# An expert-choice search without work between its steps, one pass of places, and shared experts beside the scatter

## The chip, the cores and the metric

The kernel runs on one NeuronCore of one Trainium2 chip. The metric is the device time of one execution in microseconds (us), lower is better; the time before is the median of three runs. Engines: PE is TensorE, DVE is VectorE, ACT is ScalarE, POOL is GpSimd, SP is the engine that issues most of the DMAs. TensorE runs at one of two levels, 1.2 or 2.4 GHz; the trace gives the granted clock of a stretch as a share of full speed, so that 0.50 is 1.2 GHz and 1.00 is 2.4 GHz.

## The reference

A two-layer decoder on x of shape (4, 512, 128), float32. Each layer is x + attention(norm x), x + cross-attention(norm x), x + feed-forward(norm x). The change touches only the feed-forward of layer 0, a mixture of 16 routed experts and 2 shared ones over 2048 tokens:

```python
logits = flat @ gate_w                                   # (2048, 16)
scores = jax.nn.softmax(logits.astype(jnp.float32), -1) + gate_b
_, topi = jax.lax.top_k(scores, K)                       # K = 2
weights = jnp.take_along_axis(logits, topi, axis=-1) * ROUTE_SCALE
capacity = math.ceil(N * K / n_experts * 1.25)           # 320

def per_expert(gid, w1, w3, w2):
    match = topi == gid
    assigned = match.any(-1)
    w_tok = jnp.sum(jnp.where(match, weights, 0.0), -1)
    wm = jnp.where(assigned, w_tok, -jnp.inf)
    vals, idx = jax.lax.top_k(wm, capacity)
    valid = assigned[idx]
    xs = flat[idx]
    y = _swiglu(xs, w1, w3, w2) * jnp.where(valid, vals, 0.0)[:, None]
    return (idx, y)
out = jnp.zeros_like(flat).at[idxs.reshape(-1)].add(ys.reshape(-1, Dx))
shared = jax.vmap(lambda w1, w3, w2: _swiglu(flat, w1, w3, w2))(sw1, sw3, sw2)
out = out + shared.mean(0)
```

Each expert takes, of the tokens that chose it, the 320 with the largest logit; between equal logits the earlier token wins.

## The kernel before, in words

Each engine has a program of its own, written by hand in the order in which it runs; semaphores (`wait_ge`, `then_inc`) tie the programs together. On DVE the helper `link` makes every instruction of a chain wait for the one before it; `blink` does the same inside the search loop. The stages of layer 0 follow one another: attention, cross-attention, then the feed-forward, and after it layer 1. X (128 partitions x 16 tiles x 128) is the residual, hT the normalised input with tokens along the columns. A token tile is 128 tokens, a batch is four tiles.

The feed-forward of layer 0 goes like this:

- **Norm and router.** DVE normalises 16 tiles (L1545). PE transposes them (L975), four to a bank of PSUM, ACT copies each bank to hT (L712). Then PE makes the logits, 16 matmuls with the tokens as weights (L1189), each passed twice since the data is float32.
- **Top two.** A DVE chain over 128x256 tiles: softmax, first and second choice, then `g_wm`, the logit where the token chose the expert and -1e30 elsewhere. PE transposes g_wm, so that the 16 experts lie along partitions (`g_wmT`), and POOL takes the maximum over all partitions (L567).
- **The search.** For each expert a threshold is sought between `g_lo` (at least 320 values reach it) and `g_hi` (fewer do). There are 16 steps, as a loop of 4 turns with 4 steps each. One step on DVE: three cuts (`g_try`, L1791), three comparisons of 256 values (L1794), a sum over the three results (`g_ge_cnt`, L1796), then, beside PE's work, three small instructions that lower g_hi (L1777 to L1779, `lower_end`); PE adds the counts of an expert's partitions (L1265, 3 columns); DVE tests them (L1799), counts the full cuts (L1800), raises g_lo (L1801) and divides the width by four (L1802). Behind its own matmul of each step PE runs one "guest": one unit of the shared experts, `shared_up` (L1197, two matmuls of 512 columns), and in half of the steps a half of `shared_down` (L1208, 8 matmuls of 128 columns). ACT takes Silu of one bank (L820) and copies the other (L821), POOL multiplies the two (L577) and adds the results to X (L586, L589).
- **The places.** Both ends go back to token order through PE (L1272). A token at or above g_hi is sure, one between the ends is tied. `places` counts how many came before: PE multiplies the mask by a triangle and by ones (L1281, L1282), DVE adds up the sums of the 16 tiles one after another (L1823, x15), then adds the triangle's result (L1824). It runs once for the tied tokens, to see which of them still fit, and once for those taken, to give them rows. Two casts write the rows (`g_row`, L1843), the second raises g_chain to 200.
- **The scatter.** POOL waits for g_chain 200 and issues 32 indirect DMAs (L596), which write the token rows to `xs_rows` in HBM, expert by expert; SP loads them back (L467), PE transposes them (L1218) and the routed experts run: L1228 up, L1238 down, four experts to a turn.

## Time and profile before

| what | value |
|---|---|
| median of 3 runs | 1634.54 us (1625.73 to 1634.92) |
| the profiled execution | 1623.32 us, its span 1621.5 us |
| granted TensorE clock, mean over the span | 0.903 |
| PE busy | 1384.9 us, 85% |
| DVE busy | 1001.7 us, 62% |
| ACT busy | 733.1 us, 45% |
| POOL busy | 565.8 us, 35% |
| the chain that ended last | PE 77%, DVE 12%, issue 3%, ACT 2%, POOL 2%, DMA 1% |

Busy shares are averages over all stages. Between 669 and 840 us after the span's start, the stretch of this feed-forward up to the first routed matmul, the engines take turns; that stretch is read from the trace row by row. "Idle" in brackets behind a row is the time for which the engine had nothing before it, and what ended it.

### The profile page before, as it was taken

To read this page: it belongs to the slowest core of one execution; us is meant where nothing else is said; L and a number is where in the kernel's file an instruction comes from. 1 tells how busy PE (TensorE), PEld (TensorE's weight loads), DVE (VectorE), ACT (ScalarE), POOL (GpSimd) and SP (SyncE) were. 2 spreads that over 40 slices of the span, in tenths; PEclk is the share of its full clock that TensorE was granted. 3 is DMA by queue.
4 is the path that set the end of the run, shared out by engine and by line. 5 is a ranking of instruction groups with operands and counts; after the bars stand their busy time and mean duration, and the time that the engine had idled before them with its cause. 6 is when DMAs were issued, how large, how long until landed. Compare 5 with 4: busy or idle time off the path is not lost.

```text
span 1621.5 us, 30956 instructions
## 1 busy us (share of the span) xinstructions
PE 1384.9 (85%) x10924; PEld 963.9 (59%) x10924; DVE 1001.7 (62%) x2374; ACT 733.1 (45%) x1487; POOL 565.8 (35%) x568
## 2 busy tenths in 40 slices
PE   4999999999999699557229458989989999949998
PEld 2566666666666466434127336766766776738887
DVE  2576676676666676488303328686786777755554
ACT  2566666666666365212003125554554555523222
POOL 1455555555555000023441236532332334211210
PEclk7899999999999899578659759999998999969999
DMA  3323100100000200000013224211211211000000
GB/s 129 113 82 100 34 26 31 34 23 34 34 23 23 59 2 1 0 1 1 7 38 98 47 48 117 54 47 28 41 48 26 41 47 29 21 1 1 0 0 26
DMA packets 91918, 61.36 MB, mean 38 GB/s; under 512 B 26841, under 2 KB 78890, under 8 KB 91830
## 3 DMA queue, kind: packets, MB, share of 16 engines
q1 hardware_dynamic: 89782, 58.88, 13.1%
q0 software_dynamic: 2048, 1.27, 0.3%
q8 instruction: 59, 0.97, 0.3%
q14 instruction: 29, 0.24, 0.1%
HBM read 21.63 MB, written 10.49 MB: 20 GB/s over the span
## 4 chain that ended last, share of the span: by engine, by line
PE 77%; DVE 12%; issue 3%; ACT 2%; POOL 2%; DMA 1%; SPq 1%; DVEq 0%; POOLq 0%; ACTq 0%
PE psum L1033 8%; PE psum L1378 8%; PE psum L1046 7%; PE psum L1023 7%; PE psum L1369 6%; PE psum L1500 6%; PE psum L1363 4%; PE psum L1390 4%; PE psum L1482 4%; PE psum L1228 2%; PE psum L1000 2%; PE psum L1009 2%; PE psum L1053 2%; PE psum L1004 2%; POOL xs_rows L596 2%
## 5 line engine op out<-in xcount | busy, mean ns | idle before, releaser
L561 POOL TENSOR_TENSOR arena<-arena,rden 128x512 f32<-128x512 f32 x256 | 260.8, 1040 | 253.1 <-DVE rden L1586 253.1
L755 ACT ACTIVATE arena<-psum,negmax 128x512 f32<-128x512 f32 x256 | 173.6, 683 | 136.2 <-DVE negmax L1577 134.9
L1959 DVE TENSOR_REDUCE negmax<-psum 128x1 f32<-128x512 f32 x256 | 165.2, 686 | 88.4 <-PE psum L1369 88.1
L1577 DVE TENSOR_REDUCE negmax<-psum 128x1 f32<-128x512 f32 x256 | 164.3, 684 | 11.2 <-PE psum L1023 7.7
L1033 PE MATMUL psum<-cst,arena 128*128 128x128 f32 x1024 | 143.9, 280 | 1.4 <-DVE arena L1572 0.5
L1033 PEld LDWEIGHTS psum<-cst,arena 128*128 128x128 f32 x1024 | 109.0, 141 | 52.8 <-issue 50.9
L1023 PE MATMUL psum<-a_qk 64*128 64x512 f32 x768 | 124.9, 430 | 0.0
L1369 PE MATMUL psum<-w,wqkv 128*64 128x208 f32 x1024 | 123.8, 365 | 0.0
L637 POOL TENSOR_TENSOR a_qblk<-a_qstack,cst 96x512 fp32r<-96x512 f32 x64 | 68.4, 1069 | 145.4 <-PE psum L1369 136.4
L1363 PE MATMUL psum<-a_kstack,a_qblk 96*128 96x512 f32 x256 | 99.2, 469 | 16.7 <-DMA a_kstack<-a_klo 16.7
L916 ACT ACTIVATE kT<-psum,negmax 128x512 f32<-128x512 f32 x64 | 44.0, 687 | 136.2 <-PE psum L1378 97.3
L1023 PEld LDWEIGHTS psum<-a_qk 64*128 64x128 f32 x768 | 63.0, 187 | 70.7 <-issue 59.9
L1500 PE MATMUL psum<-f_h,f_w 128*128 128x512 f32 x384 | 99.2, 407 | 1.5 <-DVE arena L2048 0.8
L1369 PEld LDWEIGHTS psum<-w,wqkv 128*64 128x64 f32 x1024 | 64.3, 141 | 58.6 <-issue 49.1
L1963 DVE COPY arena<-psum 128x512 f32<-128x512 f32 x128 | 87.2, 682 | 2.1 <-PE psum L1378 2.1
L953 ACT ACTIVATE arena<-psum 128x512 f32<-128x512 f32 x64 | 38.2, 597 | 104.3 <-PE psum L1500 104.3
L916 ACT ACTIVATE hst<-psum,negmax 128x512 f32<-128x512 f32 x64 | 44.0, 687 | 86.7 <-PE psum L1378 52.5
L1500 PEld LDWEIGHTS psum<-f_h,f_w 128*128 128x128 f32 x384 | 70.5, 191 | 18.8 <-DVE arena L2048 3.5
L910 ACT ACTIVATE arena<-psum 128x512 f32<-128x512 f32 x128 | 76.3, 596 | 1.6 <-PE psum L1378 1.6
L2048 DVE TENSOR_TENSOR arena<-psum,arena 128x512 f32<-128x512 f32 x64 | 44.2, 691 | 47.3 <-ACT arena L953 47.2
L1590 DVE SCALAR_TENSOR_TENSOR a_qk<-psum,a_qk 128x512 fp32r<-128x512 f32 x32 | 22.1, 692 | 74.3 <-ACT a_qk L732 74.3
L640 POOL TENSOR_TENSOR wqkv<-big_k,cst 128x512 f32<-128x512 f32 x64 | 67.3, 1052 | 0.0
(306 smaller groups left out, 2828.5 us busy)
## 6 DMA issues: line engine op xcount, KB each, us to landing
hst<-hT SPq DMA_DIRECT2D x32, 256.0 KB, 2.3
a_kstack<-a_khi SPq DMA_DIRECT2D x128, 64.0 KB, 2.0
wst<-wqkv SPq DMA_DIRECT2D x32, 192.0 KB, 2.4
w<-in_ew SPq DMA_DIRECT2D x2, 2048.0 KB, 8.6
a_kstack<-a_klo SPq DMA_DIRECT2D x64, 64.0 KB, 2.0
xs_rows<-f SPq DMA_DIRECT2D x3, 1024.0 KB, 5.6
arena<-xs_rows SPq DMA_DIRECT2D x8, 384.0 KB, 3.5
ys_rows<-wqkv SPq DMA_DIRECT2D x8, 384.0 KB, 2.6
```

Source lines behind the costliest of these rows:

```text
L561: pool.tensor_tensor(a0_p[u % 4], a0_p[u % 4], rden[:, u:u + 1].broadcast_to([P, SEQ]), ALU.mult).then_inc(a0_norm, 1)
L755: act.activation(a0_p[u % 4], bank[u % 4][:, :], ACT.Exp, bias=negmax[:, u:u + 1], accum_out=den[:, u:u + 1]).then_inc(a0_exp, 1)
L916: act.activation(ptile[n % 4], bank[n % 4][:, :], ACT.Exp, bias=negmax[:, n % 8:n % 8 + 1]).then_inc(a1_exp, 1)
L1023: mm = pe.matmul(bank[2 * (p % 2) + h][:, :], a0_qk[par][r:r + DK, q, p * P:(p + 1) * P], a0_qk[par][r:r + DK, k, :], start=(i == 0), stop ...
L1033: mm = pe.transpose(bank[4 + u % 2][:, kt * P:(kt + 1) * P], a0_p[u % 4][:, kt * P:(kt + 1) * P], ident)
L1046: mm = pe.matmul(bank[7][h * DK:(h + 1) * DK, qs], a0_vtok[par][:, kt, h * DK:(h + 1) * DK], a0_pT[par][h][:, kt, qs], start=(kt == 0), st ...
L1363: pe.matmul(bank[n % 4][:, :], qblk[:, hg, j, lg:lg + 2, :, :].rearrange("p g h l -> p (g h l)"), kstack[it % 2][:, n // 4, :], start=True ...
L1369: mm = pe.matmul(bank[n % 4][blk * HQ * LG:(blk + 1) * HQ * LG, first_key:first_key + WIN], rblk[:, hg, j, g, :, :].rearrange("p h l -> p ...
L1378: mm = pe.transpose(bank[4 + n % 2][:, kt * P:(kt + 1) * P], ptile[n % 4][:, kt * P:(kt + 1) * P], ident)
L1500: mm = pe.matmul(bank[2 * (u % 2) + w][:, :], w_parts[:, e, wp, w * FF + hf * P:w * FF + (hf + 1) * P], h_parts[hp][:, c * SEQ:(c + 1) * S ...
L1577: dve.tensor_reduce(negmax[:, u:u + 1], bank[u % 4][:, :], AX.X, ALU.max, negate=True).then_inc(a0_max, 1)
L1959: dve.tensor_reduce(negmax[:, n % 8:n % 8 + 1], bank[n % 4][:, :], AX.X, ALU.max, negate=True).then_inc(a1_max, 1)
```

## The change

Five edits, all in layer 0's feed-forward:

1. **Router by batch.** PE makes the logits of a batch behind the transposes of the next one, rather than all behind all.
2. **Mask.** g_wm is made with two instructions in place of three (a minimum of the logit and +-1e30).
3. **Search.** The guests are gone. Each comparison sums its own result (a second operation and an output for the accumulator), so that L1796 goes; the test of the counts sums too, so that L1800 goes; the width is divided while PE works.
4. **Places.** Sure and tied tokens lie side by side in one tile (`g_kind`, 512 columns), and one pass counts both: ones first, then the triangle. A tied token stands behind all sure ones (`g_back`); its place alone tells whether it fits.
5. **Shared experts.** All 16 units run behind the places' matmuls on PE, Silu on ACT, and the multiply and the add to X on DVE, both straight from PSUM, after g_chain 200. The ACT copies and POOL's multiplies are gone. The product tile now has two buffers (arena 1 and 2). POOL's memsets and its two staging copies stand ahead of its maximum.

```diff
             for i in range(BISECT):
                 pe.wait_ge(b_count, i + 1)
                 pe.matmul(bank[2][:, 0:CUTS], same_expert, g_ge_cnt[:, :], start=True, stop=True).then_inc(b_total, 1)
-                shared_up(i)
-                if i >= 4 and i % 4 in (1, 2):
-                    shared_down(i // 4 - 1, i % 4 == 1)
...
             pe.wait_ge(g_chain, 100)
-            pe.matmul(bank[1][:, 0:E0], ones[:, :], g_cnt[:, :], start=True, stop=True)
...
+            kinds = arena[:, 2, 1, :]
+            pe.matmul(bank[3][:, :], ones[:, :], kinds, start=True, stop=True).then_inc(g_mm, 1)
+            pe.matmul(bank[2][:, :], tri, kinds, start=True, stop=True).then_inc(g_mm, 1)
+
+            for u in range(4 * B):
+                shared_up(u)
+                if u >= 4 and u % 4 in (1, 2):
+                    shared_down(u // 4 - 1, u % 4 == 1)
...
                 for k in range(BSTEPS):
                     par = k % 2
...
                     for c in range(CUTS):
-                        ins = dve.tensor_scalar(g_ge[:, c, :], g_wmT[:, :], g_try[:, par, c:c + 1], None, ALU.is_ge)
-                    blink(ins)
-                    dve.tensor_reduce(g_ge_cnt[:, :], g_ge[:, :, :], AX.X, ALU.add).then_inc(b_count, 1)
+                        ins = dve.tensor_scalar(g_ge[:, c, :], g_wmT[:, :], g_try[:, par, c:c + 1], None, ALU.is_ge, ALU.add, g_ge_cnt[:, c:c + 1])
+                    ins.then_inc(b_count, 1)
+                    blink(dve.tensor_scalar(g_step[:, 1 - par:2 - par], g_step[:, par:par + 1], 1.0 / (CUTS + 1), None, ALU.mult))
                     lower_end(1 - par, blink)
                     dve.wait_ge(b_total, i * BSTEPS + k + 1)
-                    blink(dve.tensor_scalar(g_full[:, par, :], bank[2][:, 0:CUTS], CAP - 0.5, None, ALU.is_ge))
-                    blink(dve.tensor_reduce(g_nfull[:, :], g_full[:, par, :], AX.X, ALU.add))
-                    dve.scalar_tensor_tensor(g_lo[:, :], g_nfull[:, :], g_step[:, 0:1], g_lo[:, :], ALU.mult, ALU.add)
-                    blink(dve.tensor_scalar(g_step[:, :], g_step[:, :], 1.0 / (CUTS + 1), None, ALU.mult))
+                    blink(dve.tensor_scalar(g_full[:, par, :], bank[2][:, 0:CUTS], CAP - 0.5, None, ALU.is_ge, ALU.add, g_nfull[:, :]))
+                    blink(dve.scalar_tensor_tensor(g_lo[:, :], g_nfull[:, :], g_step[:, par:par + 1], g_lo[:, :], ALU.mult, ALU.add))
...
+            link(dve.memset(g_slot[:, 0, :, :], 0.0))
             dve.wait_ge(g_mm, 4)
...
+            tot = bank[3][:, :].rearrange("p (t k e) -> p t k e", k=2, e=E0)
+            for t in range(1, NT):
+                link(dve.tensor_tensor(g_slot[:, t, :, :], g_slot[:, t - 1, :, :], tot[:, t - 1, :, :], ALU.add))
+            link(dve.tensor_tensor(g_back[:, :], g_slot[:, NT - 1, 0, :], tot[:, NT - 1, 0, :], ALU.add))
             dve.wait_ge(g_mm, 5)
...
+            link(dve.tensor_tensor(g_slot[:, :, :, :], g_slot[:, :, :, :], bank[2][:, :].rearrange("p (t k e) -> p t k e", k=2, e=E0), ALU.add))
+            link(dve.tensor_tensor(g_slot[:, :, 1, :], g_slot[:, :, 1, :], bcast(g_back[:, :], 1, NT), ALU.add))
+            link(dve.tensor_tensor(g_slot[:, :, :, :], g_slot[:, :, :, :], g_kind[:, :, :, :], ALU.mult))
+            link(dve.tensor_tensor(g_rt[:, :, :], g_slot[:, :, 0, :], g_slot[:, :, 1, :], ALU.add))
+            link(dve.tensor_scalar(g_sc[:, :, :], g_rt[:, :, :], float(CAP) - 0.5, float(ROWS), ALU.is_ge, ALU.mult))
+            link(dve.tensor_tensor(g_rt[:, :, :], g_rt[:, :, :], g_sc[:, :, :], ALU.add))
+            link(dve.tensor_tensor(g_rt[:, :, :], g_rt[:, :, :], g_wm[:, :, :], ALU.add))
...
+            def shared_hid(u):
+                c = u // 4
+                dve.wait_ge(sh_silu, u + 1)
+                if c >= 2 and u % 4 == 0:
+                    dve.wait_ge(sh_y, c - 1)
+                dve.tensor_tensor(sh_hidden[c % 2][:, u % 4, :], bank[5 + 2 * (u % 2)][:, :], silu[:, u % 2, :], ALU.mult).then_inc(sh_hid, 1)
+
+            def shared_add(c):
+                dve.wait_ge(sh_y, c + 1)
+                xc = X[:, c * QT:(c + 1) * QT, :]
+                dve.scalar_tensor_tensor(xc, bank[0][:, :].rearrange("p (t d) -> p t d", d=D), 1.0 / NSH, xc, ALU.mult, ALU.add).then_inc(sh_x, 1)
+
+            dve.wait_ge(g_chain, 200)
+            for u in range(4 * B):
+                shared_hid(u)
+                if u >= 4 and u % 4 == 3:
+                    shared_add(u // 4 - 1)
+            shared_add(B - 1)
             routed_turn(0, True)
```

How the order moves. First DVE, one step of the search, before:

```order
L1791 SCALAR_TENSOR_TENSOR g_try<-cst,g_step,g_lo 128x3 [waits b_chain]
...
L1794 TENSOR_SCALAR arena<-big_k,g_try 128x256 x2
...
L1796 TENSOR_REDUCE g_ge_cnt<-arena 128x3 [waits b_chain]
L1777 SCALAR_TENSOR_TENSOR g_fail<-g_full,g_try 128x3
...
L1799 TENSOR_SCALAR g_full<-psum 128x3 [waits b_total]
...
L1800 TENSOR_REDUCE g_nfull<-g_full 128x1 [waits b_chain]
...
L1801 SCALAR_TENSOR_TENSOR g_lo<-g_nfull,g_step,g_lo 128x1 [waits b_chain]
L1802 TENSOR_SCALAR g_step<-g_step 128x1
```

and the same step of the change:

```order
L1776 SCALAR_TENSOR_TENSOR g_try<-cst,g_step,g_lo 128x3 [waits b_chain]
...
L1779 TENSOR_SCALAR arena,g_ge_cnt<-big_k,g_try 128x256 x2
L1781 TENSOR_SCALAR g_step<-g_step 128x1
...
L1762 SCALAR_TENSOR_TENSOR g_fail<-g_full,g_try 128x3 [waits b_chain]
...
L1784 TENSOR_SCALAR g_full,g_nfull<-psum 128x3 [waits b_total]
...
L1785 SCALAR_TENSOR_TENSOR g_lo<-g_nfull,g_step,g_lo 128x1 [waits b_chain]
```

Both reduces are gone, and the division of the width stands ahead of the wait for PE (b_total). Then PE from the search on, before:

```order
L1265 MATMUL psum<-g_ge_cnt,cst 128x3 [waits b_count]
L1197 MATMUL psum<-hT,w 128x512 [waits sh_upc]
L1197 MATMUL psum<-hT,w 128x512
L1208 MATMUL psum<-w,arena 128x128 [waits sh_hid]
L1208 MATMUL psum<-w,arena 128x128 x7
L1265 MATMUL psum<-g_ge_cnt,cst 128x3 [waits b_count]
```

and of the change:

```order
L1258 MATMUL psum<-g_ge_cnt,cst 128x3 [waits b_count] x16
L1262 MATMUL psum<-cst,big_k 128x128 [waits g_chain]
L1262 MATMUL psum<-cst,big_k 128x128
L1267 MATMUL psum<-arena,ones 128x512 [waits g_chain]
L1268 MATMUL psum<-arena,cst 128x512
L1187 MATMUL psum<-hT,w 128x512 x4
L1187 MATMUL psum<-hT,w 128x512 [waits sh_hid]
```

The 16 small matmuls follow one another, and the first two shared units (x4) stand right behind the places, with no wait. On POOL, what stands ahead of the scatter in the change:

```order
L572 MEMSET big_q 128x2048
L572 MEMSET big_k 128x2048
L573 MEMSET wqkv 128x4x64
L575 COPY arena<-w 128x512 x2
L577 ISA
L577 ISA g_all<-g_abs 128x1
L583 DMA xs_rows<-ln_h,g_row 6144x128 x32
```

where before 16 multiplies and 4 adds of 128x512 stood between the maximum and the scatter.

## Rows read from the trace of the kernel before

**Rows 1.** Timeline, norm and router: start, duration, engine, line, operation, count, [idle, releaser].
```profile
670.25 4.19 PE L975 MATMUL psum<-cst,ln_h 128*128 128x128 f32 x16 [5.04 <-DVE ln_h L1545]
675.22 6.98 PE L1189 MATMUL psum<-gw,hT 128*128 128x16 f32 x32 [0.78 <-ACT hT L712]
```

**Rows 2.** Timeline, the first two steps of the search, which no other engine's work crosses.
```profile
696.73 0.22 DVE L1791 SCALAR_TENSOR_TENSOR g_try<-cst,g_step,g_lo 128x3 f32<-128x3 f32 x1 [0.20 <-DVE g_full L1773]
...
700.24 0.22 DVE L1791 SCALAR_TENSOR_TENSOR g_try<-cst,g_step,g_lo 128x3 f32<-128x3 f32 x1
700.50 0.88 DVE L1794 TENSOR_SCALAR arena<-big_k,g_try 128x256 f32<-128x256 f32 x3
701.41 0.95 DVE L1796 TENSOR_REDUCE g_ge_cnt<-arena 128x3 f32<-128x768 f32 x1
702.28 0.15 DVE L1777 SCALAR_TENSOR_TENSOR g_fail<-g_full,g_try 128x3 f32<-128x3 f32 x1
...
702.95 0.16 DVE L1799 TENSOR_SCALAR g_full<-psum 128x3 f32<-128x3 f32 x1
...
703.65 0.22 DVE L1791 SCALAR_TENSOR_TENSOR g_try<-cst,g_step,g_lo 128x3 f32<-128x3 f32 x1
```

**Rows 3.** Timeline, a crossed step, the loop's last instruction and what follows it.
```profile
703.91 1.89 DVE L1794 TENSOR_SCALAR arena<-big_k,g_try 128x256 f32<-128x256 f32 x3
704.08 1.31 POOL L577 TENSOR_TENSOR arena<-arena 128x512 f32<-128x512 f32 x1 [9.96 <-ACT arena L821]
...
768.72 0.94 DVE L1777 SCALAR_TENSOR_TENSOR g_fail<-g_full,g_try 128x3 f32<-128x3 f32 x1 [0.21 <-DVE g_step L1802]
```

**Rows 4.** Waits between 697 and 795 us: who waited for whom, us in total, times, longest.
```profile
DVE g_try L1791 <- DVE g_step L1802: 1.5, 3, 0.5
```

**Rows 5.** Groups by line and shape: busy us, mean ns, idle before.
```profile
L755 ACT ACTIVATION_READ_ACCUMULATOR arena<-psum,negmax 128x1 f32 x256 | 50.2, 196 | 0.0
...
L820 ACT ACTIVATE arena<-psum 128x512 f32<-128x512 f32 x16 | 9.6, 601 | 66.9 <-PE psum L1197 48.8 <-POOL arena L577 18.1
...
L2048 DVE TENSOR_TENSOR arena<-psum,arena 128x512 f32<-128x512 f32 x64 | 44.2, 691 | 47.3 <-ACT arena L953 47.2
```

**Rows 6.** Timeline, the places.
```profile
775.15 0.42 DVE L1816 TENSOR_TENSOR arena<-arena 128x256 f32<-128x256 f32 x1
...
777.07 1.06 PE L1282 MATMUL psum<-arena,ones 128*128 128x256 f32 x2
...
785.76 3.04 DVE L1823 TENSOR_TENSOR arena<-arena,psum 128x16 f32<-128x16 f32 x15
...
793.46 0.17 DVE L1843 CAST g_row<-g_m 128x16 uint32<-128x16 f32 x1
```

**Rows 7.** Timeline, the scatter's first issue and the first routed matmuls.
```profile
794.61 1.31 POOL L596 DMA_INDIRECT xs_rows<-ln_h,g_row  x1 [2.20 <-DVE g_row L1843]
...
840.30 1.51 PE L1218 MATMUL psum<-cst,arena 128*128 128x128 f32 x6 [50.11 <-DMA arena<-xs_rows]
```

**Rows 8.** Groups of POOL's indirect DMAs: the scatter, and the gathers beside layer 1.
```profile
L596 POOL DMA_INDIRECT xs_rows<-ln_h,g_row x32 | 31.4, 982 | 11.6 <-issue 9.4 <-DVE g_row L1843 2.2
...
L610 POOL DMA_INDIRECT big_q<-ys_rows,g_row x16 | 16.4, 1024 | 17.5 <-DMA ys_rows<-wqkv 13.8 <-issue 3.7
```

**Rows 9.** The chain that ended last: start, length, a shared unit and a half of the down product.
```profile
721.14 1.82 PE psum L1197 x4
722.97 1.78 PE psum L1208 x16
...
735.81 3.62 PE psum L1197 x4
```

**Rows 10.** Windows: start:end, length, busy us of PE, PEld, DVE, ACT, POOL; then granted clock.
```profile
735.10:739.50 4.40, 4.24 (x7) 1.63 (x7) 4.01 (x14) 0.03 (x1) 1.33 (x2) 0.50 0.00 0
...
840.30:844.30 4.00, 4.00 (x11) 2.87 (x12) 0.98 (x2) 0.01 (x1) 0.00 (x0) 0.50 0.29 79
857.70:865.60 7.90, 7.90 (x49) 6.22 (x48) 2.86 (x6) 2.73 (x6) 1.23 (x2) 1.00 0.52 146
```

More of the change, by code:

```diff
@@ L228, in decoder_kernel @@
         arena0 = arena[:, 0, :, :].rearrange("p a b -> p (a b)")
-        sh_up = arena0[:, 2 * SEQ:4 * SEQ].rearrange("p (u t) -> p u t", u=2)
-        sh_out = featsT[:, :]
+        sh_hidden = [arena[:, 1 + i, :, :] for i in range(2)]
         g_tiles = arena[:, 2, :, :].rearrange("p a (b t e) -> p (a b) t e", b=2, e=E0)
@@ L852, in _ @@
             for u in range(4 * B):
-                shared_unit(u)
-                if u >= 6 and u % 4 == 2:
-                    shared_out(u // 4 - 1)
-            shared_out(B - 1)
+                shared_silu(u)
             routed_turn(0, True)
@@ L1190, in router, with norm_turn, norm_router @@
                 mm.then_inc(g_mm, 1)
+            def norm_turn(layer, b):
+                pe.wait_ge(ln_ready, layer * B + b + 1)
+                for t in range(QT):
+                    mm = pe.transpose(bank[4 + b][:, t * P:(t + 1) * P], ln_h[:, b * QT + t, :], ident)
+                mm.then_inc(ln_tp, 1)
+            def norm_router(layer, b, w, n):
+                pe.wait_ge(ln_out, layer * B + b + 1)
+                for t in range(b * QT, b * QT + QT):
+                    mm = pe.matmul(bank[0][:, t * n:(t + 1) * n], hT[:, t * P:(t + 1) * P], w, start=True, stop=True)
+                if b == B - 1:
+                    mm.then_inc(g_mm, 1)
             def shared_up(u):
@@ L1252, in routed_turn @@
                     routed_down(e, k, first)
-            norm_layer(F0)
             pe.wait_ge(ld_f0, 160)
-            router(F0, gw0[:, :], E0)
+            norm_turn(F0, 0)
+            for b in range(1, B):
+                norm_turn(F0, b)
+                norm_router(F0, b - 1, gw0[:, :], E0)
+            norm_router(F0, B - 1, gw0[:, :], E0)
             pe.wait_ge(g_chain, 60)
@@ L1275, in _ @@
             pe.wait_ge(g_chain, 100)
-            pe.matmul(bank[1][:, 0:E0], ones[:, :], g_cnt[:, :], start=True, stop=True)
-            def places(mask):
-                m = mask.rearrange("p t e -> p (t e)")
-                pe.matmul(bank[2][:, 0:NT * E0], tri, m, start=True, stop=True)
-                pe.matmul(bank[3][:, 0:NT * E0], ones[:, :], m, start=True, stop=True).then_inc(g_mm, 1)
-            places(g_t1[:, :, :])
-            pe.wait_ge(g_chain, 150)
-            places(g_sc[:, :, :])
+            kinds = arena[:, 2, 1, :]
[5 more added lines that the diff above has]
+                    shared_down(u // 4 - 1, u % 4 == 1)
             for first in (True, False):
@@ L1814, in _ @@
-            link(dve.tensor_reduce(g_cnt[:, :], g_t2[:, :, :].rearrange("p t e -> p e t"), AX.X, ALU.add))
-            left = upto(100)
-            dve.tensor_tensor(g_t1[:, :, :], g_t1[:, :, :], g_t2[:, :, :], ALU.subtract).then_inc(g_chain, left)
-            def places(into):
-                tot = bank[3][:, 0:NT * E0].rearrange("p (t e) -> p t e", e=E0)
-                link(dve.memset(into[:, 0, :], 0.0))
-                for t in range(1, NT):
-                    link(dve.tensor_tensor(into[:, t, :], into[:, t - 1, :], tot[:, t - 1, :], ALU.add))
-                link(dve.tensor_tensor(into, into, bank[2][:, 0:NT * E0].rearrange("p (t e) -> p t e", e=E0), ALU.add))
@@ L1834, in _ @@
-            dve.wait_ge(g_mm, 5)
-            places(g_rt)
-            link(dve.scalar_tensor_tensor(g_rt[:, :, :], bcast(iota, 1, NT), float(PITCH), g_rt[:, :, :], ALU.mult, ALU.add))
-            link(dve.tensor_scalar(g_t1[:, :, :], g_sc[:, :, :], -float(ROWS), float(ROWS), ALU.mult, ALU.add))
-            link(dve.tensor_tensor(g_rt[:, :, :], g_rt[:, :, :], g_t1[:, :, :], ALU.add))
+            sure, tied = g_kind[:, :, 0, :], g_kind[:, :, 1, :]
+            link(dve.tensor_tensor(sure, g_wm[:, :, :], bcast(bank[1][:, P:P + E0], 1, NT), ALU.is_ge))
```

83 lines of the change are left out of this document (30 added, 53 removed).

## The prediction, made before the changed kernel was run
> **What bounds the kernel now.** I read the rows in the order of the program. Up to 669 us and from 840 us on nothing is changed, and no row there belongs to a sum below except as a price. Between them no single engine bounds: the work goes from hand to hand, so what counts is which instruction the next one waits for. Four parts follow one another. (a) PE makes transposes and logits from 670.25 to 682.20 [rows 1]. (b) DVE runs its chain of top two. (c) The search runs from 696.73 to 768.72, 72.0 us [rows 2, 3]. (d) The places run from 768.72 to the end of the last cast, 793.46 + 0.17 = 793.63, 24.9 us [rows 3, 6]; then POOL scatters and the routed experts start at 840.30, 46.7 us after that cast, in which PE and DVE have next to nothing to do [rows 7].
>
> What the reader is to see in [rows 2]: two steps that nobody crosses take 3.51 us (696.73 to 700.24) and 3.41 us (to 703.65). Sixteen such steps are 16 x 3.46 = 55.4, with 1.5 us for three turns of the loop [rows 4] and 0.2 at its end 57.1. The search takes 72.0. The other 14.9 us are lost where guests cross it, in two ways: PE is busy with a guest when the count comes, and DVE instructions grow beside POOL's multiply (three comparisons 1.89 us beside it, 0.88 without; [rows 2, 3]).
>
> **The change, part by part.**
>
> *Router.* PE is the limit. Before: 11.95 us in all. Of these the transposes are spread over 4.19 us since DVE delivers a batch every 1.05 us, and the logits take 6.98 us [rows 1]. After: two batches of transposes (2.1), then 6.98 us of logits with the other two batches between them (2.1), together 11.1. That gives -0.9 us. ACT's copy of 0.60 us, priced by a like one [rows 5], hides behind the next transposes. Bounds 0 and -1.8.
>
> *Mask.* One instruction of 128x256 goes, 0.42 us by a like one [rows 6], and its wait: -0.5 us. POOL's memsets and copies now stand ahead of its maximum, while DVE and POOL have nothing to do and PE makes logits [rows 1]. Nothing.
>
> *Search.* One step, put together from the second of [rows 2]. The cuts: 700.24 to 700.50, 0.26. The three comparisons: 0.88 before, now each with its own sum. The reduce behind them, 0.87 from start to start (701.41 to 702.28), goes. Then PE: from the end of the count (702.36) to the test at 702.95 it took 0.59 us; DVE has four small instructions of its own in that time now, and four took 702.95 to 703.65 = 0.70, so DVE's 0.72 is the longer. Test and new g_lo: two of those four, 0.36, and the sum of the test, for which I take 0.10.
>
> The price of a comparison that sums is in no row. Below: as now, 0.29, with the sum for nothing. Above: 0.42, the time of a 128x256 instruction without the faster pace [rows 6], and behind it a read of the accumulator as long as ACT's, 0.20 [rows 5], fully serial: 0.62. I take 0.48: the main part 0.38, between 0.42 and the 0.34 to which instructions overlap with no wait between them (0.95 long, 0.87 apart), and 0.10 for the read, half of ACT's row, as ACT's is the nearest row and a part of it should lie beside the next instruction. With 0.10 more for the last read to land, the three are 1.54.
>
> A page speaks against the cheap end. The Trainium skill (SBUF — State Buffer, "Who interferes with whom") says that a tensor_scalar which also writes its accumulator doesn't enter the two-port mode, and (VectorE: DVE Perf Modes, "Two Vector instructions with no wait between them") that such an instruction is two. No run here shows it yet; by it the lower end falls away and the value lies between 0.42 and 0.62.
>
> Step: 0.26 + 1.54 + 0.72 + 0.46 = 2.98. Sixteen are 47.7, with 1.7 for the loop 49.4. The search gives 72.0 - 49.4 = **-22.6 us**, of which 14.9 are the guests. Bounds: at 0.29 and no read a step is 0.26 + 0.88 + 0.72 + 0.36 = 2.22, in all 37.2, -34.8; at 0.62 it is 0.26 + 1.86 + 0.72 + 0.56 = 3.40, in all 56.1, -15.9.
>
> *Places.* After, from the loop's end: three small links 0.55; two copies of 128x128 0.5; PE there and back 0.5; three of 128x256 at 0.45, 1.35; PE's 512 columns of ones at the low clock, two times the 1.06 of 256 columns [rows 6], 2.15, beside which three DVE instructions hide; 15 running sums of 32 columns, 3.04 for 16 columns [rows 6], 3.3 (the triangle's matmul hides beside them); one small, 0.2; two of 128x512 at 0.73 [rows 5], 1.45; four of 128x256 and one at 0.33, 2.2; two times product, sum and cast, 2.2. Sum 14.4, so **-10.5 us**. The second running sum (3.04 us) and the second trip to PE are the core of it; some 3 us come from POOL's and DVE's quarrel ending (0.94 us for an instruction that takes 0.15 alone; [rows 2, 3]). Bounds -8 and -12.
>
> *Scatter and shared experts.* Time T is the last cast; PE must be free at T + 46.7. PE's first two units need no DVE: they start behind the triangle, some 14.4 - 2.9 - 3.9 = 7.6 us before T, and take 2 x 3.62 at the low clock [rows 9], so they are covered. After T: the first product 0.8; 14 units of 1.82 and 6 halves of 1.78 [rows 9] are 25.5 + 10.7; then Silu, product and the add before the last down product, 0.60 + 0.69 + 0.69 [rows 5] with gaps 2.2; and two halves, 3.6. PE is free at T + 42.8, 3.9 us early. Per unit ACT needs 0.6 and DVE 0.7, so neither holds PE's 1.82. The first 4 us may run at the low clock, as at 840.30 [rows 10]; that costs 2 us and is still covered. A gather beside attention has rows of 1.02 us against the scatter's 0.98 [rows 8]: 32 x 0.04 = 1.3 at most, 0 at least, I take +0.7. PE comes to the routed experts busy: 4.00 us at 0.50 there [rows 10] would be 2 at full clock, so 0 to -2, I take -1. Together -0.3.
>
> **Sum:** -0.9 - 0.5 - 22.6 - 10.5 - 0.3 = -34.8 us. Against the profiled execution (1623.3) that is 1588.5; that execution lay 11.2 us under the median of 1634.5. Against the median it is 1599.7; I forecast **1600 us**.
>
> **The rivals.**
>
> *The sums are free.* If comparisons keep 0.29 and the read hides, the search gives 12.2 us more: 1588. For it: the reduce was a whole instruction of 0.95 us, and ACT's read has a row of only 0.20 [rows 2, 5]. Against: the page above, and two results of one instruction. 0.15.
>
> *DVE holds up POOL's descriptors.* DVE's 16 products and 4 adds now run beside the scatter. If each stopped POOL for its 0.69 us, that is 20 x 0.69 = 13.8: 1614. For it: DVE and POOL did stretch one another in [rows 3]. Against: [rows 8], gathers beside DVE's reduces and copies from PSUM are 0.04 us longer. The Trainium skill (SBUF — State Buffer, "The 'DVE blocks DMA' trap (SWDGE)") has the mechanism: a two-port DVE instruction locks GpSimd out of descriptor writing; products and adds here read PSUM, which by that page isn't such a mode, and the price by it is 0. 0.08.
>
> *The guests were not the cause.* If the 14.9 us stay (another wait in the loop), 1615. Against: both mechanisms have rows. 0.06.
>
> *PE stays at the low clock beside the scatter.* This one ends slower. The place is PE between T and the routed experts; at 3.62 a unit and 3.56 a half it is 0.8 + 50.7 + 21.4 + 2.2 + 7.1 = 82.2, so 35.5 beyond the scatter, and the -1 is gone too: 1636.5, 2 us slower than before. It costs from 1.10 times the full-clock work on (43.7 / 39.8), and passes the time before at 1.93 times. For it: the search leaves PE nearly idle for 50 us, and a unit at 735.81 ran at 0.50 [rows 9, 10]. Against: dense work at 857.70 runs at 1.00 [rows 10], and after 50 us idle the low level lasted 4 us of work [rows 7, 10]. 0.04.
>
> **How the numbers follow.** The forecast has the other 0.67. The range goes from 1580 (cheap comparisons, and a median of after that falls where the profiled execution of before did) to 1614 (dear comparisons at 1607, or a held-up scatter). A measurement of this kernel can tell about 1%, 16 us, from no change, so faster by over 1% means under 1618: all cases but the last, and part of the bad ends, 0.93. Within 1%: 0.05. Slower: 0.02, for two bad ends together.
>
> **What would show it.** Right: a step of 3.0 us in every turn of the loop, with comparisons of about 0.42 and a row for the accumulator's read; 49 us from first cuts to the loop's end; 14.4 us from there to the last cast, with one row of 15 running sums; POOL's issues still 0.98 us long; the last half of down done 2 to 4 us before the first routed transposes, which still wait for the DMA. Wrong: a wait for PE of over 0.8 us in the steps; DVE or ACT late in the shared units; routed transposes that wait for PE's own down product. It would be wrong as a whole if PE ended the scatter stretch.

## The result, and the profile after

The changed kernel takes 1618.75 us in the median (1618.26 to 1624.41, 5 runs; the kernel before beside it 1634.92, 1625.73 to 1639.27): 0.9934 of the time before, 95% interval 0.9905 to 0.9963. That is 16 us or 0.7% less; I had forecast 1600 us, 34.8 less, and a range up to 1614. The profiled execution took 1618.75 us, its span is 1617.0.

The stages from the router to the first routed matmul, in both profiled executions. T is the end of the last cast, R the start of the first routed transposes:

| stretch | before | after | moved | forecast |
|---|---|---|---|---|
| start of the stage (first ln_h row) | 669.08 | 669.86 | +0.8 | 0 |
| norm and router, to DVE's copy of the logits | 13.2 us | 11.6 us | -1.6 | -0.9 |
| top two and mask, to the first cuts | 14.4 | 14.0 | -0.4 | -0.5 |
| search [rows 2, 3] | 72.0 | 46.5 | -25.5 | -22.6 |
| places, to T [rows 6] | 24.9 | 15.05 | -9.9 | -10.5 |
| T to R [rows 7] | 46.7 | 75.7 | **+29.0** | -0.3 |
| R | 840.30 | 832.70 | -7.6 | |

Behind R nothing is changed, yet it took 781.2 us before and 784.3 after. In 18 profiled executions it lay between 781 and 794 us, and the first cuts came between 690.2 and 697.4. So one execution says little within 10 us, and the experiments are read by R - T, with the times beside it. R - T comes from the one profiled execution of each run, the time from all of its executions.

*The search.* One step in the timeline after; it answers to [rows 2]:

```profile
701.16 0.22 DVE L1776 SCALAR_TENSOR_TENSOR g_try<-cst,g_step,g_lo 128x3 f32<-128x3 f32 x1
701.41 0.48 DVE L1779 TENSOR_SCALAR_CACHE_REDUCE arena<-big_k,g_try 128x256 f32<-128x256 f32 x1
701.82 0.08 DVE L1779 DVE_READ_ACCUMULATOR arena<-big_k,g_try 128x1 f32 x1
701.82 0.47 DVE L1779 TENSOR_SCALAR_CACHE_REDUCE arena<-big_k,g_try 128x256 f32<-128x256 f32 x1
...
702.75 0.59 PE L1258 MATMUL psum<-g_ge_cnt,cst 128*128 128x3 f32 x2 [2.21 <-DVE arena L1779]
...
703.95 0.22 DVE L1776 SCALAR_TENSOR_TENSOR g_try<-cst,g_step,g_lo 128x3 f32<-128x3 f32 x1
...
741.93 0.16 DVE L1762 SCALAR_TENSOR_TENSOR g_fail<-g_full,g_try 128x3 f32<-128x3 f32 x1 [0.21 <-DVE g_lo L1785]
```

A step takes 703.95 - 701.16 = 2.79 us, no DVE row waits over 0.2 us for PE in the whole loop, and the loop ends at 741.93 where it ended at 768.72.

*The places*, answering to [rows 6] and the first line of [rows 7]:

```profile
745.38 2.08 PE L1267 MATMUL psum<-arena,ones 128*128 128x512 f32 x2 [1.57 <-DVE arena L1798]
...
747.56 3.29 DVE L1806 TENSOR_TENSOR wqkv<-wqkv,psum 128x32 f32<-128x32 f32 x15 [1.42 <-PE psum L1267]
...
756.80 0.18 DVE L1820 CAST g_row<-g_m 128x16 uint32<-128x16 f32 x1
...
757.95 1.31 POOL L583 DMA_INDIRECT xs_rows<-ln_h,g_row  x1 [65.10 <-DVE g_row L1820]
```

*Where the time went.* T is 756.98, 36.65 us earlier than before, and POOL scatters at its old pace (32 rows of 984 ns; [rows 8] had 982). Then the timeline shows this:

```profile
769.01 1.88 PE L1187 MATMUL psum<-hT,w 128*128 128x512 f32 x4
...
770.73 1.95 PE L1198 MATMUL psum<-w,arena 128*128 128x128 f32 x16
...
772.52 1.88 PE L1187 MATMUL psum<-hT,w 128*128 128x512 f32 x4
...
774.37 0.60 ACT L807 ACTIVATE arena<-psum 128x512 f32<-128x512 f32 x1 [6.34 <-remote]
...
775.00 0.69 DVE L1831 TENSOR_TENSOR arena<-psum,arena 128x512 f32<-128x512 f32 x1 [6.25 <-issue]
...
775.75 1.98 PE L1187 MATMUL psum<-hT,w 128*128 128x512 f32 x4 [1.35 <-issue]
...
797.91 0.97 POOL L583 DMA_INDIRECT xs_rows<-ln_h,g_row  x1 [0.31 <-issue]
800.09 34.06 SPq L469 DMA_DIRECT2D arena<-xs_rows  x3
803.24 1.08 ACT L807 ACTIVATE arena<-psum 128x512 f32<-128x512 f32 x2 [28.27 <-remote]
...
804.61 3.78 PE L1187 MATMUL psum<-hT,w 128*128 128x512 f32 x4 [26.88 <-DVE arena L1831]
```

Unit 6 of the shared experts (counted from 0) stands on PE from 769.01 to 770.89; its Silu, which waits for nothing else, starts at 774.37. Unit 7 is done by 774.40, its Silu starts at 803.24, together with that of unit 8 (x2). From 777.73, when unit 8 ends, to 803.24 neither PE, ACT nor DVE computes. PE's own wait is for DVE's product, DVE's for ACT's Silu, and ACT's for a signal of PE that should have come 28.8 us earlier; the profile finds no releaser for it ("remote") and the chain of waits has it as a stretch of its own:

```profile
757.76 9.65 PE psum L1187 x16
767.45 6.89 another core or an unknown queue
774.39 28.82 another core or an unknown queue
803.24 0.61 ACT arena L807
```

When the signals come, seven of the 16 units and three of the four down products are still to do, 29 us, with the scatter over. The routed transposes, which waited for the load before [rows 7], now wait for PE's own queue. Where DVE and ACT signal inside this stretch, it is in time: ACT's Silu ends at 774.97 and DVE starts at 775.00, DVE's product ends at 775.69 and PE starts at 775.75. Of the 29 us some 2 are the clock: after the gap TensorE is granted 0.50 from 804 to 808 us, and the unit at 804.61 takes 3.78 us.

### The profile page after: what moved, and what is told of

Its sections match the earlier page's. It is cut to its first block, busy times and chain, and to the rows that moved or that the text cites. A ratio compares the mean times of both kernels' runs of the same rounds, so it can differ in the third digit from the quotient of the medians.

```text
span 1617.0 us, 30906 instructions
## 1 busy us (share of the span) xinstructions
PE 1384.9 (86%) x10918; PEld 965.4 (60%) x10918; DVE 986.2 (61%) x2407; ACT 724.8 (45%) x1467; POOL 541.2 (33%) x548
## 3 DMA queue, kind: packets, MB, share of 16 engines
q1 hardware_dynamic: 89782, 58.88, 13.2%
## 4 chain that ended last, share of the span: by engine, by line
PE 77%; DVE 13%; another core or an unknown queue 2%; issue 2%; ACT 2%; DMA 1%; SPq 1%; POOL 0%; DVEq 0%; POOLq 0%; ACTq 0%
PE psum L1010 8%; PE psum L1365 7%; PE psum L1023 7%; PE psum L1000 7%; PE psum L1356 6%; PE psum L1487 6%; PE psum L1350 4%; PE psum L1377 4%; PE psum L1469 4%; PE psum L1218 2%; PE psum L977 2%; PE psum L986 2%; PE psum L981 2%; PE psum L1030 2%
## 5 line engine op out<-in xcount | busy, mean ns | idle before, releaser
L1350 PE MATMUL psum<-a_kstack,a_qblk 96*128 96x512 f32 x256 | 99.1, 469 | 14.6 <-DMA a_kstack<-a_klo 14.6
L930 ACT ACTIVATE arena<-psum 128x512 f32<-128x512 f32 x64 | 38.3, 598 | 104.3 <-PE psum L1487 104.3
L887 ACT ACTIVATE arena<-psum 128x512 f32<-128x512 f32 x128 | 76.2, 596 | 1.6 <-PE psum L1365 1.6
L807 ACT ACTIVATE arena<-psum 128x512 f32<-128x512 f32 x16 | 9.4, 597 | 133.3 <-PE psum L1187 97.6
```

The source lines that it names most:

```text
L1350: pe.matmul(bank[n % 4][:, :], qblk[:, hg, j, lg:lg + 2, :, :].rearrange("p g h l -> p (g h l)"), kstack[it % 2][:, n // 4, :], start=True ...
```

## The experiments

Theory S: the scatter holds back what TensorE signals. Rival O: a place in TensorE's or ACT's own program does, such as the crossing from one block of its instructions to the next, whatever runs beside it. The summary first; each run follows with its edit:

| run | R - T | time, median | ratio to before, 95% |
|---|---|---|---|
| the change | 75.7 | 1618.75 | 0.9934 (0.9905 to 0.9963) |
| scatter behind the shared experts | 90.7 | 1638.52 | 1.0038 (1.0001 to 1.0075) |
| scatter 12 us later | 77.9 | 1624.79 | 0.9953 (0.9916 to 0.9990) |
| quarter of the down product | 59.0 | 1607.48 | 0.9826 (0.9747 to 0.9905) |
| half of the scatter | 53.6 | 1594.55 | 0.9772 (0.9694 to 0.9850) |
| gathers for scatters | 67.9 | 1611.78 | 0.9882 (0.9833 to 0.9930) |
| an eighth of the rows | 75.7 | 1618.30 | 0.9917 (0.9881 to 0.9953) |
| plain DMAs of SP | 43.3 | 1587.22 | 0.9744 (0.9690 to 0.9798) |
| memsets for the DMAs | 48.2 | 1595.99 | 0.9755 (0.9724 to 0.9786) |
| one pause | 66.4 | 1612.13 | 0.9850 (0.9805 to 0.9896) |
| three pauses | 51.7 | 1598.34 | 0.9795 (0.9748 to 0.9843) |
| two pauses | 54.0 | 1595.01 | 0.9765 (0.9731 to 0.9799) |
| last chunk moved | 60.3 | 1604.89 | 0.9846 (0.9796 to 0.9896) |
| three waits for products | 57.4 | 1603.63 | 0.9842 (0.9792 to 0.9891) |
| three waits, chunk moved | 52.4 | 1602.92 | 0.9827 (0.9779 to 0.9877) |
| two pauses, chunk moved | 49.9 | 1594.30 | 0.9749 (0.9717 to 0.9780) |
| search with the old count | 75.5 | 1630.70 | 0.9992 (0.9960 to 1.0025) |

### Is it the scatter?

```diff
@@ POOL, ahead of the scatter: alone
+            pool.wait_ge(sh_x, B)
@@ or, in the second run
+            pool.wait_ge(sh_hid, 6)
```

> The change, with one more wait: POOL starts the scatter only when the last shared chunk has been added to X. In the changed kernel TensorE's signals for units 6, 7 and 8 and for the first down product came 3.5, 28.8, 25.5 and 22.8 us after the modelled ends of their matmuls, all inside the scatter. Theory S (the scatter holds TensorE's signals back): alone, the shared stage runs at the forecast pace, PE is free some 43 us after the last cast (T), the scatter takes 43 us and the load 4 behind it, so the routed transposes start at T + 91 against T + 77 in the change: 14 us slower than the change, about 1633 us, and no gap above 4 us on ACT in the shared stage. Rival O (a place in TensorE's or ACT's own program, whatever runs beside it): the gap of 29 us stays, routed transposes at T + 124, about 1665 us.

R - T is 90.7, as S has it. TensorE's last down product ends at 795.65, 43.4 us behind T (752.23); the forecast's working said 42.8. Left alone, the shared stage is as I had costed it. O is out by 33 us.

> The change, with POOL's scatter started only after the sixth product of the shared experts, some 12 us later than in the change. Theory S: units 0 to 5 and more pass undisturbed, the late signals come after the scatter has begun, at a later unit than 6, and end with the scatter; routed transposes near T + 75, time within 6 us of the change. Rival O: the gap stands at units 6 and 7 as before and the scatter ends inside the work after it.

The gap moved with the scatter, past units 6 to 9 (now at 770.98 to 777.91), and ended 4.6 us behind the end of its last row:

```profile
769.85 1.31 POOL L584 DMA_INDIRECT xs_rows<-ln_h,g_row  x1 [76.80 <-issue]
...
787.17 0.60 ACT L808 ACTIVATE arena<-psum 128x512 f32<-128x512 f32 x1 [8.66 <-remote]
...
809.75 0.97 POOL L584 DMA_INDIRECT xs_rows<-ln_h,g_row  x1 [0.30 <-issue]
...
815.33 1.08 ACT L808 ACTIVATE arena<-psum 128x512 f32<-128x512 f32 x2 [27.56 <-remote]
```

That excludes O a second time: the program of PE and ACT is word for word that of the change. The Trainium skill (Runtime: NRT & Kernel Launch, "Instruction fetch mechanics") calls the cost of crossing from one block of instructions to the next mostly hidden. By that page O was unlikely, and these two runs agree.

### Of what does it depend on TensorE's side and on the length?

```diff
@@ PE, shared_down: a quarter of it
-                    for k in range(4):
+                    for k in range(1):
@@ in the other run, POOL: half of the scatter
-            for t in range(NT):
+            for t in range(NT // 2):
```

> The change with a quarter of the shared experts' down product (one of four k terms; the other three are left out), so TensorE issues 16 instead of 64 matmul records per chunk there. Theory S in the form that dense TensorE work beside the scatter is what backs up: the signals stay in time, ACT has no gap over 4 us, PE is free near T + 35 and the scatter's end sets the routed start at about T + 47: some 30 us faster than the change, near 1589 us. If only the scatter matters and not TensorE's density, a gap until the scatter's end stays: routed start at T + 65 to 70, some 8 us faster.

Neither form of S as written: R - T is 59.0, between the 47 and the 65 to 70. The longest gap on ACT is 16.95 us instead of 28.27, with shorter ones of 3.65 and 5.75 ahead of it. How much TensorE does beside the scatter matters, but lighter work doesn't escape.

> The change with half of the scatter (the tokens of the second half are left out: 16 indirect DMAs instead of 32, SP waits for those 16). Theory S: the held signals come when the half scatter ends, some 20 us earlier than in the change, so the routed transposes start at T + 57 and the time is about 1598 us. Rival O: the gap has its 28.8 us as before, time as the change, 1618 us.

R - T fell to 53.6 and the time to 1594.6, somewhat better than expected. The gaps shrink to 5.79 and 7.34 us, and the last ends at 775.73, behind the 16th issue at 772.21.

### What in the scatter?

```diff
@@ POOL: gathers, with the same row numbers
-                    pool.indirect_dma_start(xs_rows, bass.IndirectOffsetOnAxis(ap=g_row[:, c, t:t + 1], axis=0), ln_h[:, t, :], None,
+                    pool.indirect_dma_start(gathered[c][:, t, :], None, xs_rows, bass.IndirectOffsetOnAxis(ap=g_row[:, c, t:t + 1], axis=0),
@@ or few rows
-                                            bounds_check=ROWS - 1, ...
+                                            bounds_check=ROWS // 8 - 1, ...
@@ or SP writes the blocks
+            for n in range(2 * NT):
+                if n and n % 2 == 0:
+                    sp.wait_ge(scattered, 16 * n)
+                sp.dma_start(xs_rows[n * P:(n + 1) * P, :], ln_h[:, n // 2, :]).then_inc(scattered, 16)
@@ or POOL only fills memory
+            for n in range(24):
+                if n:
+                    pool.wait_ge(scattered, n)
+                pool.memset(gathered[0], 0.0).then_inc(scattered, 1)
```

> The change with the direction of the 32 indirect DMAs turned: POOL gathers rows of xs_rows into SBUF by the same row numbers instead of scattering tokens (the scatter is left out, the routed experts see unsorted rows). POOL's instructions and the shared experts are the same. If any indirect DMA of POOL holds back TensorE's signals (S1), the gap on ACT stays and the routed transposes start near T + 77 as in the change (1619 us). If it is the writing of rows to DRAM (S2), TensorE's signals come in time, the units keep 1.82 us each and the routed start falls to about T + 47: about 1589 us.

Mostly S1: gaps of up to 15.63 us stay with no row written to HBM, though R - T is 67.9 and not 77. S2 is out as the whole cause. Here signals came through in the middle of the row too, at 783.41 and 790.40; why gathers hold less than the scatter was not found.

> The change with the scatter's bound cut to an eighth of the rows: POOL issues its 32 indirect DMAs as before, and only tokens of the first two experts are written (the others are left out). If POOL's own work on descriptors holds TensorE (S3), the gap stays as long as POOL issues, T + 77. If it is the traffic of rows (S1 or S2), the gap goes or shrinks to an eighth: routed start near T + 47, about 1589 us.

S1 and S2, as traffic of rows, are out. With an eighth of the rows R - T is 75.7, to the tenth that of the change, and the gap is 28.19 us:

```profile
798.51 0.97 POOL L583 DMA_INDIRECT xs_rows<-ln_h,g_row  x1 [0.30 <-issue]
...
803.82 1.08 ACT L807 ACTIVATE arena<-psum 128x512 f32<-128x512 f32 x2 [28.19 <-remote]
```

The amount that is moved has no part in it. But this run does not single out S3. In the pages of the two profiles (packets, MB, share) the software queue, which serves scatter and gathers, moves half the bytes in as many packets as before:

```profile
q0 software_dynamic: 2048, 1.27, 0.3%
```
```profile
q0 software_dynamic: 2048, 0.66, 0.2%
```

So POOL's own work and what that queue does with its packets were not separated.

> The change without POOL's scatter: SP writes the same 32 blocks of 128 rows of 512 B into xs_rows with plain DMAs of its own queue, two at a time, each pair behind the landing of the pair before (row order left out). That is the same amount written to DRAM in about 16 x 2.3 = 37 us, with no indirect DMA. If DRAM writes of rows hold TensorE's signals, a gap of some 20 us on ACT remains; if it is POOL's queue (S1 or S3), no gap over 4 us, and TensorE ends the stretch at about T + 44: about 1587 us.

The same bytes written by SP's queue hold nothing: R - T is 43.3, the 42.8 at which the forecast had TensorE free. Waits of ACT in this run, 750 to 800 us, and below it in the changed kernel, 750 to 833 us (us in total, times, longest). The 6.7 is the wait for unit 2, which PE starts only behind DVE's first product at T, and no late signal, though I had written no gap over 4:

```profile
ACT arena L809 <- PE psum L1189: 33.4, 15, 6.7
```
```profile
ACT arena L807 <- PE psum L1187: 97.6, 12, 66.2
ACT arena L807 <- remote: 34.6, 2, 28.3
```

> The change with the 32 indirect DMAs replaced by 24 memsets of 128x2048 on POOL, one behind the other, 1.83 us each by the row of such a memset in the changed kernel, 44 us in all (the scatter is left out). If any POOL instruction in a row holds TensorE's signals, the gap on ACT stays at some 29 us and the time is the change's, 1619 us. If it is POOL's issuing of indirect DMAs, no gap over 4 us, POOL's end and TensorE's end fall together near T + 45 to 48: about 1588 us.

A POOL that is busy for 44.65 us in a row holds nothing either; all 16 waits of ACT are put down to PE and there is no "remote":

```profile
758.73 44.65 POOL L585 MEMSET big_q<- 128x2048 f32 x24 [64.20 <-DVE g_row L1821]
...
803.40 5.57 SPq L469 DMA_DIRECT2D arena<-xs_rows  x3
806.84 1.51 PE L1209 MATMUL psum<-cst,arena 128*128 128x128 f32 x6 [4.17 <-DMA arena<-xs_rows]
```

So it is the indirect DMAs that POOL issues, and not a busy POOL. R - T is 48.2 as expected; the time of 1596 us is 8 above my 1588, and T itself was late here (758.66).

### Does a pause let the signals out?

```diff
@@ POOL, x_landing: behind every 8 DMAs
             for t in range(NT):
+                if t and t % 4 == 0:
+                    pool.wait_ge(scattered, 32 * t)
@@ one pause: t in (8,); two: t in (5, 10)
@@ v_groups: the wait is for products instead
+                    pool.wait_ge(sh_hid, (6, 10, 14)[t // 4 - 1])
```

> The change with POOL's scatter in four groups of eight indirect DMAs; before the second, third and fourth group POOL waits for the 6th, 10th and 14th product of the shared experts. In the runs so far TensorE's signals are in time in the first 13 us of a row of indirect DMAs and come again when the row ends. If what holds them builds up while POOL issues one after the other and is gone once POOL pauses (theory S3), each pause lets them out within 1 to 3 us, the shared experts keep pace, and the routed start falls to T + 50 to 54: 1591 to 1596 us. If only the end of the whole scatter lets them out, every wait adds to it: slower than the change, over 1619 us.

Better than the change by 15 us, but short of what I expected, by 3 to 7 us in R - T (57.4) and by 8 to 13 in the time, with gaps of 5.46 and 7.33 us on ACT in the third group. At the first two borders the product was there almost at once, so POOL stood for only 1.1 us (starts 2.35 us apart instead of 1.28), and in the third group signals were late as in a longer row. At the last border the product was itself late, and POOL stood from 792.3 to 801.2. So the scatter ended late, and PE waits 2.29 us for the load in the end.

> The change with the same four groups, but POOL waits at each border only until its own DMAs so far have landed (some 1.3 us of pause after the last issue), whatever the shared experts do. If a short pause alone lets TensorE's signals out, as v_groups, 1591 to 1598 us. If they need longer than 1.3 us of pause, the gap stays for a large part, and the time lies near the change's, 1610 to 1622 us.

Right: R - T is 51.7, and the routed transposes wait for the load again, which answers to [rows 7]:

```profile
776.78 0.60 ACT L809 ACTIVATE arena<-psum 128x512 f32<-128x512 f32 x1 [4.05 <-PE psum L1189]
...
791.64 3.81 PE L1200 MATMUL psum<-w,arena 128*128 128x128 f32 x32 [2.10 <-DVE X L1838]
...
797.94 0.97 POOL L585 DMA_INDIRECT xs_rows<-ln_h,g_row  x1 [0.30 <-issue]
798.98 0.69 DVE L1838 SCALAR_TENSOR_TENSOR X<-psum,X 128x512 f32<-128x512 f32 x1 [7.48 <-remote]
800.11 5.76 SPq L469 DMA_DIRECT2D arena<-xs_rows  x3
...
803.73 1.51 PE L1210 MATMUL psum<-cst,arena 128*128 128x128 f32 x6 [8.28 <-DMA arena<-xs_rows]
```

Pauses of 1.6 to 1.7 us are enough behind rows of eight (the starts at the borders are 2.90 to 2.98 us apart instead of 1.28), where two of 1.1 us were not, in one profiled execution each. One late signal is left, in the last group: the down product ends at 795.45 and DVE adds it at 798.98, where it costs nothing.

> The change with one pause of the x_landing kind in the middle of the scatter (16 indirect DMAs, landing, 16 more). The hold-up sets in some 13 us after the first issue of a row, or 10 DMAs; a half of 16 takes 20.4 us, so signals are late for some 7 us in each half, and the second half ends with units left over. Between x_landing (1598 us) and the change (1619 us): about 1604 us. If the pauses did not matter but something else in x_landing did, as the change.

Rows of 16 are too long: 66.4, 1612 us, 8 above my number, with gaps of 10.7 us in the first half and 15.4 in the second, where I had 7. The signal held in the first half came at 780.55, 3.7 us behind the end of its last row and 1.8 us into the second half.

How long the signals take behind the end of a row's last DMA grows with the row: 1.1 to 1.7 us for rows of 10 and 12 in the next run, 2.5 to 3.7 for rows of 16, 4.3 to 4.6 for the full scatter of the change, of the eighth of the rows and of the later start; the run with the moved chunk, below, is an exception. A backlog that has to drain would look like this; that it is one was not shown.

> x_landing with two pauses, behind 10 and 20 indirect DMAs, instead of three. If a row of 10 is still inside the first 13 us, one pause of 1.6 us less: 1597 us. If rows of 12.8 us are already too long, late signals leave TensorE work over behind the scatter: 1600 us or above.

R - T is 54.0, 2.3 more than with three pauses, since TensorE ends the stretch again (a gap of 5.0 us in the row of 10 and 7.2 in the last row of 12); the times, 1595.0 and 1598.3, don't tell the two apart.

### The last chunk elsewhere, alone and with pauses

```diff
@@ PE, behind the routed experts (ACT and DVE alike)
-            for u in range(4 * B):
+            for u in range(4 * (B - 1)):
...
             routed_down(E0 - 1, 3, False)
+            for u in range(4 * (B - 1), 4 * B):
+                if u % 4 == 1:
+                    pe.wait_ge(r_yc, E0)
+                shared_up(u)
+            for first in (True, False):
+                shared_down(B - 1, first)
```

> The change with the last chunk of the shared experts (four units and a down product, 4 x 1.82 + 2 x 1.78 = 10.8 us of TensorE) moved behind the routed experts, where TensorE has nothing to do for 23 us while POOL gathers the first batch (896.6 to 920.1 in the changed kernel). What is left after the scatter falls from 29 to 18 us; if gathers don't hold TensorE's signals, nothing is paid behind: 11 us faster than the change, about 1608 us. If gathers hold them too, the layer norm's transposes behind come later by the same 11 us or more and the time is that of the change, 1619 us or above.

R - T is 60.3, so 15.4 less, and the time 14 us under the change. The chunk is 10.8 of them; the other 4.6 are luck as far as is known, since the held signals came earlier, at T + 39.8 instead of T + 46.3, and ahead of the last issue:

```profile
791.58 0.60 ACT L807 ACTIVATE arena<-psum 128x512 f32<-128x512 f32 x1 [23.92 <-remote]
...
792.74 0.97 POOL L583 DMA_INDIRECT xs_rows<-ln_h,g_row  x1 [0.30 <-issue]
```

So the end of the row is not what lets them out. TensorE's next work behind the chunk still waits for the layer norm of DVE (11.03 us idle), so eight gathers beside the chunk show no harm. The part behind R took 790.7 us, inside the spread of 781 to 794, so a few us lost there can't be excluded.

> Both remedies: the scatter in four groups (waits for the 6th, 10th and 12th product) and the last shared chunk behind the routed experts. If v_groups works, TensorE is free before the scatter's end and the routed start is set by the scatter, the pauses and the load: T + 48 to 50, 1588 to 1591 us. If pauses do nothing, the time is v_gap's, 1605 us, or above.

TensorE is free before the load, as expected (it waits 7.81 us for it), but R - T is 52.4, 2 to 4 us above, and the time 1602.9, 12 above. Two gaps of 8.2 and 5.2 us stand on ACT again: the pause at the second border was only 0.2 us (starts 1.49 us apart), and at the third POOL stood 4.7 us for a late product.

> v_two_pauses with the last shared chunk behind the routed experts, so TensorE has 10.8 us less to do beside the scatter. If v_two_pauses still has TensorE work over behind the scatter, this takes it away: 1594 to 1597 us. If the scatter sets the routed start anyway, no gain over v_two_pauses (within 2 us), or a loss where the chunk meets the gathers.

R - T is 49.9 and the load releases PE again, so the scatter, its pauses and the load are now the bound. 1594.3 us is the fastest of the kernels that leave nothing out, 0.9749 of the time before, but not told apart from two pauses alone (0.9765).

### What the search gained by

```diff
@@ DVE, one step: the sums undone
-                        ins = dve.tensor_scalar(g_ge[:, c, :], ..., None, ALU.is_ge, ALU.add, g_ge_cnt[:, c:c + 1])
-                    ins.then_inc(b_count, 1)
+                        ins = dve.tensor_scalar(g_ge[:, c, :], ..., None, ALU.is_ge)
+                    blink(ins)
+                    dve.tensor_reduce(g_ge_cnt[:, :], g_ge[:, :, :], AX.X, ALU.add).then_inc(b_count, 1)
```

> The change with the old form of the count in the search: three comparisons without a sum and one reduction behind them, no guests. A step takes the 2.80 us of the change, less three comparisons of 0.48 and their reads, plus 0.88 and 0.87: about 3.1 to 3.2 us, so the search is 5 to 6 us longer (46.5 to about 52) and the time 5 to 6 us above the change's 1619. If the guests had not been the cause of the search's waits, a step would be near the 4.5 us of before and the search near 72 us.

A step is 3.36 us, the search 694.91 to 750.69 = 55.8 us. So without guests, with the old count, it is 16.2 us shorter than before, and the sums give another 9.3 (I had expected 5 to 6). The time, 1630.7, is 12 above the change's and not told apart from before (0.9992): with R - T at 75.5 the scatter stretch takes back what the guests' removal and the one pass of places give. Groups of this run, and below them the two groups of the change (busy us, mean ns):

```profile
L1781 DVE TENSOR_REDUCE g_ge_cnt<-arena 128x3 f32<-128x768 f32 x16 | 15.2, 953 | 0.5
L1779 DVE TENSOR_SCALAR arena<-big_k,g_try 128x256 f32<-128x256 f32 x48 | 14.1, 349 | 0.8 <-DVE g_try L1776 0.2
```
```profile
L1779 DVE TENSOR_SCALAR_CACHE_REDUCE arena<-big_k,g_try 128x256 f32<-128x256 f32 x48 | 20.5, 476 | 0.7
L1779 DVE DVE_READ_ACCUMULATOR arena<-big_k,g_try 128x1 f32 x48 | 4.0, 83 | 0.0
```

## Why the prediction was wrong

**Router and mask** lie inside their bounds: the router gave -1.6 us against -0.9, the mask -0.4 against -0.5.

**The search** was right in kind and 2.9 us too small. The search without guests and with the old count is 16.2 us shorter; some 1.6 of it are the division beside PE and the test that sums (a step of 3.36 us against the 3.46 of an uncrossed one before), so the guests are worth 14.6, where I had 14.9. A comparison that sums is 0.476 us long, as I took it (0.48), but the next starts 0.40 us behind it, since its tail and the read of 0.083 us overlap, so three cost 1.21 and not 1.54. From there to the test it was 0.87 and not 0.72, which takes half of that back. The step is 2.79, not 2.98. My rival of free sums is out: 0.349 us without, 0.476 with. The Trainium skill (VectorE: DVE Perf Modes, "Two Vector instructions with no wait between them") calls such an instruction two. The trace agrees, with a row for the read.

**The places** were right: -9.9 against -10.5.

**Scatter and shared experts** is the step that failed, by 29.3 us. I wrote "Per unit ACT needs 0.6 and DVE 0.7, so neither holds PE's 1.82" and summed durations to "PE is free at T + 42.8"; it was free at T + 75.9 (832.87). The sum itself holds: 43.4 us from T with the scatter out of the way, 43.3 with plain DMAs, against 42.8. What fails is the assumption that another engine hears of an instruction's end when it ends. While POOL issues indirect DMAs in a long row, TensorE's signals come up to 28.8 us late. My row for the two working side by side was the gathers [rows 8], which I read for POOL's pace only, and they stand in rows of eight; the scatter's row of 32 had, before, nobody beside it [rows 7: idle 50.11]. So no row of before had the case, and I should have bounded it instead of taking +0.7.

**The rivals.** None of mine was it. DVE does not hold POOL's descriptors (984 ns each, pitch 1.28 us as before). TensorE was not kept at the low clock: granted 0.50 from 757 to 760 us, 0.53 to 763, and 1.00 from 763 to 778. The range's upper end, 1614, was made from priced mishaps; the condition that I named for being wrong as a whole, "if PE ended the scatter stretch", is what happened.

**Where the 18.75 us come from.** Against the profiled execution of before I had 1588.5, and the changed kernel's profiled execution took 1618.75, which is 30.3 more: 29.3 from this step, 3.9 from the start of the stage and the part behind R, 0.7 from places and mask, less 3.6 from search and router. That the forecast of 1600 missed by only 18.75 is luck: I had added 11.2 us, since the profiled execution of before lay that far under its median, and that of the change lies on its median.

**What stays open.** Why POOL's indirect DMAs do this, whether through POOL's own work or the software queue's packets, and whether it is the completion of the matmul or its signal that is late. In rows of 8 DMAs with 1.6 us between them signals are at most 3.5 us late, with rows of 10 and 12 gaps of 5.0 and 7.2 us appear, with rows of 16 gaps of 5.8 to 15.4, with the row of 32 one of 28.3, and lighter work of TensorE suffers less; whether it is a count of DMAs or a time was not separated. Every execution on record, profiled or not, has a span and a granted clock, so there is none without tracing, and whether the tracing of TensorE's many instructions takes part was not tested. That ACT's and DVE's signals are spared was seen here only while they had little to signal. Of the 3.1 us by which the part behind R was longer than before, no cause was found, and executions differ by more.

## What to carry to other kernels

Empty time beside a long row of indirect DMAs on POOL is not free time for TensorE: in this kernel, work of TensorE whose results others wait for is held there, while the same work alone, or beside SP's plain DMAs, keeps its pace. Break the row by letting POOL wait for its own DMAs' landing every eight or so (1.6 us each; 24.0 of the 29.0 us came back in R - T, 20.4 in the time); don't make it wait for the work that is being held. When a prediction puts two engines side by side for the first time, look in the trace for a row of that pair at that length, and if there is none, price the overlap's failure as a case: the gain is then what remains if the stretches run one behind the other.

## What the runs showed that I had not expected

- TensorE's signals up to 28.8 us late beside 32 indirect DMAs in a row on POOL; none late beside 24 memsets (44.65 us) or beside 32 plain DMAs of SP.
- The number of rows moved has no effect: an eighth of them, in as many packets, gives the same R - T, 75.7 us.
- Pauses of 1.6 us between rows of eight clear it, two of 1.1 us did not. Behind longer rows the signals take longer to come, 4.3 to 4.6 us behind 32 DMAs, and once they came before the row's end.
- Two comparisons with sums start 0.40 us apart though each row is 0.476 us long.
